# A long convolution and a mixture of experts on one core: normalised rows kept with channels innermost, taps and decays in four buffers

## The reference

```python
def attn(x, delta, alpha, beta, gamma, omega):       # x already normalised, (b, l, d)
    p = sigmoid(delta); q = 1.0 - p * sigmoid(alpha)
    vander = t[None, None, :] * log(q)
    kernel = p * beta * exp(vander)                  # (d, n, l), n = 16
    k = einsum('dnl,dn->dl', kernel, gamma * sqrt(1.0 / 16))
    out = irfft(rfft(x) * rfft(k))[..., :l]          # causal convolution along l
    return out + x * omega
x = x + attn(layernorm(x), ...)
x = x + moe(layernorm(x), ...)
for e in range(8):                                   # moe
    h = gelu(xr @ w1A[e].T @ w1B[e]); ye = h @ w2A[e].T @ w2B[e]
    out = out + mask_e * ye
y = zeros.at[tok].add(weight * out)                  # two experts per token
```

## Time and profile before

| | before |
|---|---|
| median of three runs | 1257.15 us |
| the profiled execution | 1263.37 us |
| its span | 1261.3 us |
| busy: TensorE, VectorE, ScalarE, GpSimd | 954.1, 909.8, 842.9, 617.4 us |
| moved by DMA | 287.88 MB, mean 228 GB/s |
| first half of the convolution | about 129 to 430 us of the span |
| experts | about 430 to 929 us |
| second half, and the last stores | about 929 to 1229, to 1261 us |

### The profile page before, as it was taken

One profiled execution on the slowest core, in us unless ns is written; L12 is line 12 of the kernel. 1 busy time (PEld: TensorE's weight loads), 2 busy tenths in 40 slices (PEclk: granted clock), 3 DMA queues, 4 the chain that ended last, 5 costly groups with the idle time before them and its releaser, 6 DMA issues.

```text
span 1261.3 us, 34527 instructions
## 1 busy us (share of the span) xinstructions
PE 954.1 (76%) x11452; PEld 770.1 (61%) x11452; DVE 909.8 (72%) x1495; ACT 842.9 (67%) x1191; POOL 617.4 (49%) x755
## 2 busy tenths in 40 slices
PE   3740787768778849999999899998978776776780
PEld 2520676656666736777777677776756665665660
DVE  6978898758769527777777777775469885775880
ACT  4841787758668726767766667667678776675870
POOL 4142886647545126666766666665553232231320
PEclk9975899889879969999999999999989898887995
DMA  7998957979979899999998898884368599898909
GB/s 247 326 387 293 226 132 207 273 178 288 272 193 282 275 280 278 261 252 267 238 226 232 200 226 229 228 200 107 82 155 187 141 286 233 228 267 182 283 17 266
DMA packets 337535, 287.88 MB, mean 228 GB/s; under 512 B 18088, under 2 KB 285000, under 8 KB 336962
## 3 DMA queue, kind: packets, MB, share of 16 engines
q1 hardware_dynamic: 293698, 212.01, 61.3%
q0 software_dynamic: 19520, 36.26, 14.7%
q10 hardware_dynamic: 24256, 38.81, 9.2%
HBM read 197.41 MB, written 100.61 MB: 236 GB/s over the span
## 4 chain that ended last, share of the span: by engine, by line
PE 27%; SPq 20%; DMA 12%; issue 11%; DVE 8%; ACT 2%; POOL 1%; POOLq 1%; DVEq 1%; ACTq 0%
SPq L641 8%; PE ps L1440 7%; DMA wide<-y_d,pick_g 7%; SPq L618 7%; PE ps L1453 6%; DMA wide<-taps_d 4%; PE ps L1346 3%; SPq L683 3%; DVE xb L1158 3%; PE ps L1358 2%; PE ps L1413 2%; PE ps L1465 2%; PE ps L1425 2%; PE ps L1333 2%; SPq L686 1%
## 5 line engine op out<-in xcount | busy, mean ns | idle before, releaser
L1346 PE MATMUL ps<-xn,wb 128*128 128x128 f32 x2048 | 294.1, 303 | 46.5 <-ACT wb L885 46.4
L1346 PEld LDWEIGHTS ps<-xn,wb 128*128 128x128 f32 x2048 | 268.1, 211 | 65.7 <-ACT wb L885 51.2
L512 POOL TENSOR_TENSOR cen<-xb,mean 128x512 f32<-128x512 f32 x128 | 142.2, 1111 | 270.3 <-DVE state L1174 218.5
L951 ACT ACTIVATE cen<-ps 128x1024 f32<-128x1024 f32 x156 | 155.9, 1021 | 136.5 <-PE ps L1440 120.4
L1148 DVE TENSOR_TENSOR xn<-cen,rstd 128x1024 f32<-128x1024 f32 x128 | 171.5, 1340 | 58.2 <-POOL cen L512 43.3
L878 ACT ACTIVATE wb<-wide 32x1024 f32<-32x1024 f32 x128 | 145.9, 1140 | 88.5 <-DMA wide<-taps_d 71.0
L1333 PE MATMUL ps<-xn,near 128*32 128x128 f32 x2048 | 89.8, 297 | 146.2 <-DVE xn L1148 75.4
L1440 PE MATMUL ps<-carry,wb 64*128 64x256 f32 x1248 | 169.9, 402 | 26.6 <-DVE carry L1221 26.3
L1158 DVE TENSOR_TENSOR xb<-xb,ps 128x1024 f32 (+1 forms) x128 | 152.8, 1194 | 14.0 <-PE ps L1358 13.8
L1453 PE MATMUL ps<-cen,xn 128*64 128x128 f32 x2496 | 161.1, 277 | 0.9 <-ACT cen L951 0.8
L1453 PEld LDWEIGHTS ps<-cen,xn 128*64 128x64 f32 x2496 | 136.7, 137 | 39.7 <-ACT cen L951 19.9
(11 more groups left out here) (164 smaller groups left out, 1352.7 us busy)
## 6 DMA issues: line engine op xcount, KB each, us to landing
out<-xb SPq DMA_DIRECT2D x116, 512.0 KB
xb<-L_attn_x SPq DMA_DIRECT2D x96, 512.0 KB
xb<-L_attn_x SPq DMA_DIRECT2D x32, 1024.0 KB, 9.7
xb<-L_attn_x ACTq DMA_DIRECT2D x128, 256.0 KB
wb<-L_ffn_w_B SPq DMA_DIRECT2D x78, 256.0 KB
wide<-taps_d SPq DMA_DIRECT2D x62, 256.0 KB
y_d<-xb SPq DMA_DIRECT2D x16, 512.0 KB
dk<-decay_d SPq DMA_DIRECT2D x62, 128.0 KB
```

Source lines behind the costliest of these rows:

```text
L512: pool.tensor_tensor(cen[:, k, 0:UC // 2].rearrange("p d r -> p r d"), unit_view(pool, g, i, k)[:, :, 0:UC // 2], mean[:, g * P:(g + 1) * ...
L951: act.activation(act_h[:, b % 2].rearrange("p f t -> p (f t)"), ps[:, 2 * (b % 2):2 * (b % 2) + 2, :].rearrange("p a t -> p (a t)"), ACT.G ...
L1346: ins = pe.matmul(ps[:, QB * k + b, d * P:(d + 1) * P], wb[:, h, k * QB + b, d, :], xn[:, k, 2 * b + d, :], start=(b > 0 and d == 0), stop ...
```

## The change

`cen` and `xn` become `[partition, k, column, channel]`: the eight channels of a unit are adjacent, as in `xb`. The centring on GpSimd and VectorE writes runs of four floats, the scaling repeats each column's 1/deviation for eight adjacent elements, and TensorE reads its 128 columns with a step of eight floats.

Taps now have four quarters of `wide` and decays four buffers `dk`, each with its own semaphore. ScalarE fetches blocks 0 to 3 before the first tile, and SyncE from then on fetches the block after next but one (`i + 3`) where it fetched the next. ScalarE's loop runs over four blocks instead of two. Stores are counted on one semaphore for each of the 16 pieces. GpSimd's centring of the second half is written out instead of looped.

```diff
-        dk = sb("dk", [P, 2, N * KD])
+        dk = sb("dk", [P, WB, N * KD])
-        cen = sb("cen", [P, 2, UC, P])
-        xn = sb("xn", [P, 2, UC, P])
+        cen = sb("cen", [P, 2, P, UC])
+        xn = sb("xn", [P, 2, P, UC])
...
                 wait(pool, s_loc, 2 * (i - 1))
-                wait(pool, s_dk, 16 * (i + 1))
+                wait(pool, s_dk[i % WB], 16 * (i // WB + 1))
...
-                        pool.tensor_tensor(cen[:, k, 0:UC // 2].rearrange("p d r -> p r d"),
+                        pool.tensor_tensor(cen[:, k, :, 0:UC // 2],
...
-                if g == 0:
-                    for i in range(NK):
-                        centre(i, i == 0, i == NK - 1)
-                else:
-                    over_tile_blocks(pool, g, lambda i, begin, end: centre(i, isinstance(i, int) and i == NK, end))
+                for i in range(g * NK, (g + 1) * NK):
+                    centre(i, i == g * NK, i == (g + 1) * NK - 1)
...
-                        y_done, o_done = stored(j)
-                        wait(sp, s_first, y_done)
-                        wait(sp, s_out, o_done)
+                        wait(sp, s_put[j], 16 * stored(j))
...
-                turned, placed = 2 * (i - 1), i - 1
-                kept = 16 * i
-                now(sp, turned, placed, kept)
+                turned, placed = 2 * (i - WB + 1), i - WB + 1
+                now(sp, turned, placed)
                 wait(sp, s_rev, turned)
...
-                    if not (first and b == 0) and not (final and b == BT - 1):
-                        load_weights(t * BT + b + 1, (b + 1) % 2)
+                    if not (first and b == 0) and not (final and b + WB > BT):
+                        load_weights(t * BT + b + WB - 1, (b + WB - 1) % WB)
...
-            for h in range(2):
-                row = taps_d[h:h + 1].rearrange("k s i d -> k (s i d)")
+            for k in range(WB):
+                row = taps_d[k:k + 1].rearrange("k s i d -> k (s i d)")
...
-                wait(act, s_w[h], 16 * (i // 2 + 1))
+                wait(act, s_w[m], 16 * (i // WB + 1))
...
-                dve.tensor_tensor(cen[:, k, UC // 2:].rearrange("p d r -> p r d"),
+                dve.tensor_tensor(cen[:, k, :, UC // 2:],
...
                 dve.tensor_tensor(xn[:, k], cen[:, k],
-                                  rstd[:, g * P:(g + 1) * P][:, None, :].to_broadcast([P, UC, P]),
+                                  rstd[:, g * P:(g + 1) * P][:, :, None].to_broadcast([P, P, UC]),
                                   ALU.mult).then_inc(s_xn, 1)
...
-                                        xn[:, k, 2 * b + d, :], start=(d == 0), stop=(d == 1),
+                                        xn[:, k, :, 2 * b + d], start=(d == 0), stop=(d == 1),
...
-                                        xn[:, k, 2 * b + d, :], start=(b > 0 and d == 0), stop=False,
+                                        xn[:, k, :, 2 * b + d], start=(b > 0 and d == 0), stop=False,
```

More of the change, by code:

```diff
@@ L70, in build @@
     TB = 4
+    WB = 4
     NL = P // LR
@@ L146, in build @@
         spare = sb("spare", [P, 4])
-        cen_row = cen[:].rearrange("p k d r -> p (k d r)")
-        xn_row = xn[:].rearrange("p k d r -> p (k d r)")
+        cen_row = cen[:].rearrange("p k r d -> p (k r d)")
+        xn_row = xn[:].rearrange("p k r d -> p (k r d)")
         par = cen_row[0:NU, 0:8 * P].rearrange("p (a b) -> p a b", a=8)
@@ L250, in build @@
         s_tapd = [sem(f"s_tapd{k}") for k in range(TB)]
-        s_dk = sem("s_dk")
+        s_dk = [sem(f"s_dk{k}") for k in range(WB)]
         s_wd = sem("s_wd")
@@ L260, in build @@
         s_x = sem("s_x")
-        s_w = [sem(f"s_wk{k}") for k in range(2)]
+        s_w = [sem(f"s_wk{k}") for k in range(WB)]
         s_cen = sem("s_cen")
@@ L274, in build @@
         s_ev = sem("s_ev")
-        s_out = sem("s_out")
-        s_first = sem("s_first")
+        s_put = [sem(f"s_put{k}") for k in range(PIECES)]
         s_wl1 = sem("s_wl1")
@@ L473, in place_decays @@
             def place_decays(i):
[L475 to L479, removed]
+                dst = near[:, i % 2][:, :, 0:3:2, :]
+                src = dk[:, i % WB].rearrange("p (n s d) -> p s d n", s=SB, d=2)
                 wait(pool, s_loc, 2 * (i - 1))
-                wait(pool, s_dk, 16 * (i + 1))
+                wait(pool, s_dk[i % WB], 16 * (i // WB + 1))
                 pool.tensor_copy(dst, src).then_inc(s_wd, 1)
@@ L583, in _ @@
             pool.wait_ge(s_sf, 4)
-            pool.wait_ge(s_first, 16 * YP * DG)
+            for j in range(YP):
+                pool.wait_ge(s_put[j], 16 * DG)
             pool.wait_ge(s_yz, 16)
@@ L623, in stored @@
             def stored(g, t):
[L625 to L631, removed]
+                return lambda j: t + 1 if g == 0 or j < YP else t
             def store_tile(g, t, pieces):
@@ L637, in store_tile @@
                     if g == 0 and j < YP:
[L638 to L642 removed]
+                        dst = y_rows[:, j * PR:(j + 1) * PR, bass.ds(d0, P)]
+                    else:
+                        dst = o_rows[:, bass.ds(row, PR), bass.ds(d0, P)]
+                    sp.dma_start(dst, xb_row[:, bass.ds(r0, PR), :]).then_inc(s_put[j], 16)
             for j, a in enumerate((delta, alpha, beta)):
@@ L670, in _, with load_weights @@
             sp.wait_ge(s_keep, NL)
-            def load_weights(i, h):
+            def load_weights(i, k):
                 kb = i % NK if isinstance(i, int) else sp.snap(i % NK)
@@ L704, in tile @@
                         if b == BT // 2:
-                            sp.wait_ge(s_out, 16 * (PIECES - YP) * t)
-                            sp.wait_ge(s_first, 16 * YP * t)
+                            for j in range(PIECES):
+                                sp.wait_ge(s_put[j], 16 * t)
                         j = b - BT // 2
@@ L767, in _ @@
             sp.wait_ge(s_a, NQ)
-            load_weights(NK, 0)
-            load_weights(NK + 1, 1)
+            for k in range(WB):
+                load_weights(NK + k, k)
             sp.wait_ge(s_dv, 2 * DV_STATS)
@@ L780, in _ @@
             sp.wait_ge(s_outb, 16 * PIECES)
-            sp.wait_ge(s_out, 16 * (PIECES - YP) * (DG - 1) + 16 * PIECES * DG)
+            for j in range(PIECES):
+                sp.wait_ge(s_put[j], 16 * (NT if j < YP else NT - 1))
         @block.scalar
@@ L832, in _ @@
             act.wait_ge(s_dec, 16 * NK)
-            for h in range(2):
-                row = taps_d[h:h + 1].rearrange("k s i d -> k (s i d)")
+            for k in range(WB):
+                row = taps_d[k:k + 1].rearrange("k s i d -> k (s i d)")
                 src = bass.AP(row.tensor, row.offset, [[2, ZR], [2 * (P + ZR), SB], [1, 2 * P]])
-                wait(act, s_dk, 16 * h)
-                act.dma_start(taps_in[h * ZR:(h + 1) * ZR], src).then_inc(s_w[h], 16)
-                act.dma_start(dk[:, h, :], decay_d[h:h + 1].rearrange("k s n d -> (k s) (n d)")).then_inc(s_dk, 16)
+                act.dma_start(taps_in[k * ZR:(k + 1) * ZR], src).then_inc(s_w[k], 16)
+                act.dma_start(dk[:, k, :], decay_d[k:k + 1].rearrange("k s n d -> (k s) (n d)")).then_inc(s_dk[k], 16)
             def deviations(g):
@@ L843, in deviations, with steps @@
                                bias=eps[:, 0:1]).then_inc(s_std, 1)
-            def steps(i, h, first, final):
+            def steps(i, m, first, final):
+                h = m % 2
                 for k in range(2):
@@ L865, in steps @@
                     if not final:
-                        reverse(i + 1, k, 1 - h)
+                        reverse(i + 1, k, (m + 1) % WB)
                     if k == 0:
@@ L870, in steps, with reverse @@
                         lower(i + 1, 0, 1 - h)
-            def reverse(i, k, h):
-                dst = wb[:, h, k * QB:(k + 1) * QB]
-                src = taps_in[h * ZR:(h + 1) * ZR, k * QB:(k + 1) * QB].rearrange("p s (m d) -> p s d m", d=2)[:, :, :, ::-1]
-                wait(act, s_w[h], 16 * (i // 2 + 1))
+            def reverse(i, k, m):
+                dst = wb[:, m % 2, k * QB:(k + 1) * QB]
+                src = taps_in[m * ZR:(m + 1) * ZR, k * QB:(k + 1) * QB].rearrange("p s (m d) -> p s d m", d=2)[:, :, :, ::-1]
+                wait(act, s_w[m], 16 * (i // WB + 1))
                 wait(act, s_loc, 2 * (i - 1))
@@ L893, in reversed_first, with over_quarters @@
                 lower(g * NK, 0, 0)
-            def over_parities(g):
+            def over_quarters(g):
                 steps(g * NK, 0, True, False)
[L898 to L901, removed]
+                with act.Fori(g * NK // WB, (g + 1) * NK // WB - 1) as p:
+                    for m in range(1, WB + 1):
+                        steps(p * WB + m, m % WB, False, False)
+                for m in range(1, WB):
+                    steps((g + 1) * NK - WB + m, m, False, m == WB - 1)
             reversed_first(0)
@@ L907, in _ @@
             act.wait_ge(s_rt, NROUTE)
-            over_parities(0)
```

(3 more changed lines are left out.)

5 lines of the change are left out of this document (2 added, 3 removed).

## The result

The changed kernel takes 1401.27 us (median of four runs, 1398.28 to 1402.67) against 1256.22 for the kernel before: ratio 1.115, 95% interval 1.112 to 1.118. It is 145 us slower where I had forecast 52 us faster, and outside my range. The kind of outcome is that of rival A, which I had priced at 1375.

What follows compares the result with a forecast made beforehand. VectorE was taken to bound the first and last tiles of each half, DMA plus late taps the middle ones. Gains of 36 + 17 = 53 us from 1257.15 gave 1204, say 1205; range 1188 to 1305, the forecast's own 1190 to 1221.

Steps and rivals of the forecast that it cites:

- rival A: TensorE pays for the step of its moving operand: all eight tiles become TensorE's, 118 us slower, 1375; chance 0.29.
- What bounds the kernel: Convolution halves: VectorE bounds first and last tiles at 3.97 us per unit; middle tiles: full DMA, then 10 us nearly idle.
- 16 x 3.7 + 4 = 63: Engines' time in a tile after the change: 16 units of 3.7 us plus 4 for filling and draining.
- (1): VectorE's centring writes runs of four: 691 ns instead of 1057, a gain of 0.37 us per unit.
- (2): GpSimd's centring stays at 1.10 us for 512 elements; the layout gains nothing there.
- (3): TensorE's moving operand gets a 32-byte step: large group between 2.05 and 3.6 us, the lower taken, so no cost.
- (4): Taps and decays four blocks deep: middle tiles 74 instead of 83.15 us, 36 us gained in four, bounds 0 to 40.
- (5): Stores counted by piece, ScalarE's four-block loop, GpSimd's second half written out: 0 counted, bounds -1 to +2 us.
- my sum of 53: Total gain forecast: 36 us in the middle tiles plus 17 us in the engine-bound tiles.
- Rival B: Only part of the gain: the step costs TensorE 10 to 30 ns per instruction, or centring isn't faster; 1221 to 1245, chance 0.17.
- break-even: Surcharge of some 55 ns per large matmul instruction, from which rival A decides; 4.45 us per unit.
- Rival C: DMA engines are the limit in middle tiles: the 10 us return as a wait for rows; 1257, chance 0.04 with the like.

Runs made afterwards that it cites:

- experiment 3: The changed kernel, but TensorE alone reads adjacent columns of xn (values not computed rightly): 1209.68 us, ratio 0.960.
- experiment 5: Three versions of the changed kernel, TensorE reading xn with a step of two, three or four floats (values not right): 1205.23, 1258.96 and 1384.23 us.
- experiment 8: The kernel with channels in pairs and four buffers, TensorE loading the large group's weights with a step of eight floats (values not right): 1363.27 us, ratio 1.084.
- experiment 1: The changed kernel with the old layout of cen and xn, taps and decays still four blocks deep: 1224.38 us against 1258.34, ratio 0.972.
- experiment 6: The changed kernel with cen and xn laid out in pairs of adjacent channels, TensorE reading with a step of two floats: 1207.55 us, ratio 0.961.

## Why the prediction was wrong, step by step

**What bounds the kernel** was read rightly for the middle tiles and for the first tile of the first half, which takes 63.4 us in experiment 3, my 16 x 3.7 + 4 = 63. It was not for the last tile of a half: 68.2 and 68.7 us in experiment 3 as in the kernel before (68.3 and 68.8). The faster centring gains nothing there: the tile now starts with a wait for its rows, in which TensorE idles for 11 to 12 us (3.7 before).

**(1) VectorE's centring**: right, 684 ns against my 691. **(2) GpSimd's centring**: right, 1098 ns median in the changed kernel, 1102 before and 1096 in pairs, so the layout was never its cost.

**(3) TensorE's read is the step that failed.** I put both bounds down, 2.05 and 3.6 us for the large group, and chose the lower "since a column already lasts 1.0 ns at full clock, more than the 0.73 that a far step adds on VectorE, and it can hide there". It does not hide: the group takes 3.97 us. A piece costs 1.9 ns in experiment 5, and where every column is in a piece of its own, the pieces set the pace in place of the columns. What had to be compared with TensorE's 1.0 ns was VectorE's whole time for an element with a far step, 1.04 + 0.73 = 1.77, and not the 0.73 that it adds. That VectorE's 1.77 is the same fetch as TensorE's 1.9 is a reading that no run shows. The upper bound was that comparison and lay only 10% under the measured 3.97. So the mechanism was in the text, as rival A; what was wrong was the choice, and the chance of 0.29. The Trainium skill (SBUF — State Buffer, Specifications) says that SBUF's lines are 16 bytes and two hits in a line are needed for full bandwidth. I cited it against the change and did not follow it, for the reason quoted above. Experiment 5 agrees for TensorE's moving operand: with two columns in each piece the group is as fast as with adjacent ones (2.08 us), with 128 columns in 96 pieces an instruction takes 184 ns, so the edge lies between 1.33 and 2 hits. For the weights experiment 8 shows that a step of eight costs as much, and not where the edge is.

**(4) The buffers**: the mechanism was right, and the size, 36 us forecast and 34 measured alone, came out by luck. I had 74 us per middle tile and it is 71 to 72 in experiment 1 and 69 to 71 in experiment 6. So the middle tiles gain 44 us there, and what I had put at nothing, the rows that come late for the last tiles and the later start, takes 12 back (experiment 1).

**(5) Semaphores, loops and the first fetches**: I had 0, at most 2 us. In the four traces with two buffers the first scaling starts at 127.1 to 129.0 us, in the eight with four buffers at 130.3 to 132.6, some 3.5 later. Which part of the change does it is not shown. Experiment 3 gains 49 us, near my sum of 53, but again the parts cancel. By its trace the middle tiles gain 47 us where I had 36, the other tiles 10 where I had 17, and 4 are lost ahead of the first tile and between the halves.

**Rival A** was right in kind, and 26 us too low: the unit of TensorE is 5.60 us, not 5.4, times 16 in eight tiles. **Rival B** did not come about. The step of three floats costs 56 ns more per large instruction, above B's 10 to 30, and lands at 1259; I had put the break-even at 55 ns. **Rival C** was half right where TensorE doesn't bound: the DMA gap went, but in experiments 1, 3 and 6 the centring waits longer for rows, 80.5, 96.4 and 78.5 us on GpSimd against 42.6 before.

## What to carry to other kernels

For TensorE a float32 layout is judged by how many 16-byte pieces its access touches: a step of the moving operand is free up to 8 bytes (2.08 us for 16 instructions), costs 44% at 12 bytes and nearly doubles the instruction from 16 bytes on; for the weights 32 bytes doubled the load. VectorE's centring was equally fast with runs of two and of four floats (684 ns, against 1057 for single ones), and GpSimd's took 1.10 us in every layout. When the writer wants the channels together and TensorE wants the columns together, interleave just two of them: in experiment 6 both get full rate. When a wait in a queue is taken away, look for the transfer that is late next: here it was the rows. And where a text has two bounds for an unmeasured cost on the busiest engine, with a break-even between them, the cost belongs in the forecast until a row excludes it.

## What the hardware showed that I had not expected

The price of the step hardly depends on TensorE's clock. At the start of a middle tile of the changed kernel the granted clock is 0.51, the lower of its two levels (1.2 of 2.4 GHz), after 3.34 us in which TensorE idled. The windows row and the timeline:

```profile
1183.00:1189.00 6.00, 4.30 (x30) 3.77 (x31) 4.32 (x6) 2.94 (x4) 1.32 (x2) 0.51 0.82 231
```

```profile
1184.70 1.13 PE L1319 MATMUL ps<-xn,near 128*32 128x128 f32 x16 [3.34 <-DVE xn L1134]
1185.77 4.09 PE L1332 MATMUL ps<-xn,wb 128*128 128x128 f32 x16
...
1191.51 3.97 PE L1332 MATMUL ps<-xn,wb 128*128 128x128 f32 x16
```

It is 4.09 us at the low clock and 3.97 at the full one, where adjacent columns take 3.47 and 2.05. The first large group of each of the eight tiles took 3.99 to 4.09 us, at granted clocks from 0.50 to 0.79. So with the step the full clock brings some 3%. Over its whole run the changed kernel was granted more clock than the kernel before (0.948 against 0.911) and is the slower one all the same. I read this as a time of memory, not of the array; that is not shown, and what sets the 1.9 ns the runs don't tell.
